# A windowed-attention stack on one core: TensorE's loop by half batches, products of 64 rows, k scaled by GpSimd

## The chip, the cores and the metric

One NeuronCore of a Trainium2 chip runs the whole program; the other cores are idle. The metric is the device time of one execution in microseconds, median of repeated runs. Everything is float32, except for a few bf16 operands in the first part and the masks.

## The reference

```python
x = L0_attn_x                                  # (8, 512, 128)
xn = _layernorm(x)
x + attn(xn) + stack(xn)

def stack(x):                                  # 6 layers
    for i in range(6):
        x = attn_layer(shift_tokens(x), Wqkv[i], q_scale[i], k_scale[i], Wo[i]) + x
        x = ffn_layer(shift_tokens(x), ...) + x

def attn_layer(x, Wqkv, qs, ksc, Wo):          # 16 heads of 64
    q, k, v = split(x @ Wqkv)
    q, k = l2norm(q) * qs, l2norm(k) * ksc     # t / max(norm, 1e-12)
    q = q * cos * scale + rotate_half(q) * sin * scale
    k = k * cos / scale + rotate_half(k) * sin / scale
    # queries of a window of 32 see the keys of their window and the one before
    return local_attention(q, k, v) @ Wo
```

`attn` is plain attention with 16 heads of 8 over 512 tokens. `ffn_layer` is a layer norm, a product to 2x341, an exact gelu gate and a product back to 128.

## The kernel before, in words

Four parts run one after another: a layer norm with transposes (`layer_norm_and_transpose`), the plain attention (`global_attention`, a hardware loop over pairs of its 32 tiles, L260), the windowed stack (`windowed_stack`) and the final sum (`add_up`). The change touches only the windowed stack.

The stack works in units. A unit is one batch of one layer, 512 tokens in TPB = 4 tiles of 128, so there are 48 units. Activations lie transposed in `xT`, 128 channels on the partitions. For a tile, TensorE makes q, k and v (L1023, two matmuls of 512 columns each), 1,024 columns a tile in a PSUM slot. ScalarE squares q and k (L889), GpSimd folds the squares in two (`fold`, L749), VectorE sums them and puts a floor under the norm (`norms`, L816 and L817), ScalarE makes the reciprocal root (`norm`, L939 and L944, event `rooted`). Meanwhile VectorE multiplies q and k by the cosine and sine tables (`rotate`, L796 and L798), GpSimd adds the two (`add_q`, `add_k`, L754), and VectorE scales the sum by the root (`scale_q`, `scale_k`, both L825). TensorE transposes (`qT`, `kT`, L977), ScalarE copies out (L907, L914). Scores of a tile (`s`) are a mask matmul (L982) and 64 matmuls of 64 rows (L992); VectorE takes the maximum off (L833, L834), ScalarE exponentiates (L918), TensorE transposes the probabilities (`r`, L977), ScalarE copies (L924).

The products with the values come in two stages a tile, `va` and `vb`, for the heads' two halves (L1004). `va` holds v in the tile's own windows, `vb` the same shifted by a window of 32 rows; transfers on SyncE's queue make `vb` from `va` (L717 to L721). Both have a second dimension of 2 that is zero outside of one half of the partitions, so that one matmul with all 128 rows gives two windows side by side, 2x65 columns (64 and a column of ones that sums the probabilities). VectorE divides (L842, L843), and once both are there transposes in blocks (`turn`, L850). After the fourth tile comes the unit's own work: `wo` (L1045), `residual` (L856), a token shift (L880 and on), `centre`, `var`, `z`, the three pairs `h` (L1056) with gelu gate and `hid` (L864), and `y` (L1060, then L868).

The order on each engine is written out by hand in strings, PE_ORDER, DVE_ORDER, ACT_ORDER, POOL_ORDER and SP_ORDER; a trailing "-" means the unit before. Four PSUM slots of two banks are shared by all stages by the table SLOTS_OF; a stage on TensorE waits until the slot's last user has been read. `units` unrolls each order in a first unit, a loop over the batches of the first layer (L665), and an outer loop over layers (L667) that holds the layer's first unit and a loop over the other seven (L670).

## Time and profile before

| | |
|---|---|
| median of 3 runs | 4115.5 us (4113.0 to 4125.6) |
| profiled execution | 4122.6 us |
| its span | 4120.8 us |
| busy: TensorE / VectorE / ScalarE / GpSimd | 3682.6 / 3501.6 / 2524.6 / 1584.2 us |
| mean granted TensorE clock | 0.974 |

Times are from the start of the span. Busy time of TensorE ("PE") is that of its matmuls; weight loads ("PEld") run beside them and each matmul of float32 stands as two records (a transpose as one). A bracket "[0.68 <-issue]" says how long the engine was idle ahead of the row and what ended it; "issue" is none of the other engines. A matmul row's duration reaches past the start of the next one, so costs are read from start to start.

### The profile page before, as it was taken

The page shows a single profiled execution, that of the slowest core. Times are in us where ns is not written, and L with a number is a line of the kernel's source. Part 1 is how long each engine was busy: PE and PEld are TensorE (multiplying, and loading weights), DVE is VectorE, ACT ScalarE, POOL GpSimd, SP SyncE. Part 2 cuts the span into 40 slices and gives each one's busy share as a digit, 9 for nine tenths or more (in the row PEclk, how much of TensorE's full clock was granted, in tenths as well). Part 3 has the DMA queues.
Part 4 walks back from the last instruction along what each step waited for, and adds up shares of the span by engine and source line. Part 5 has one row for each costly group of instructions (what it writes and reads, how often), then busy time and mean ns, then how long its engine had stood idle before and what let it go on. Part 6 is the DMA issues. An engine that isn't in the chain of part 4 may idle for free. (4 is left out here: it accounts for less than half of the span.)

```text
span 4120.8 us, 121950 instructions
## 1 busy us (share of the span) xinstructions
PE 3682.6 (89%) x49057; PEld 2078.7 (50%) x49312; DVE 3501.6 (85%) x4692; ACT 2524.6 (61%) x3292; POOL 1584.2 (38%) x1114
## 2 busy tenths in 40 slices
PE   5888885799998999998999989999989999899997
PEld 2333331455555555555555545555555555555554
DVE  6788885799898898898899889898879899789985
ACT  3666663465666565656666656666656666566663
POOL 3232231434343444444444434444434343344441
PEclk8999997899999999999999999999999999999998
DMA  1000001111112111112111111111121111111112
GB/s 27 1 1 1 1 1 57 41 37 25 37 25 52 36 32 30 35 28 58 27 36 30 33 53 32 31 34 29 31 58 25 37 25 37 51 32 31 32 31 57
DMA packets 60615, 131.31 MB, mean 32 GB/s; under 512 B 15748, under 2 KB 31624, under 8 KB 60168
## 3 DMA queue, kind: packets, MB, share of 16 engines
q1 hardware_dynamic: 60168, 124.11, 12.4%
q8 instruction: 432, 7.08, 0.7%
q14 instruction: 15, 0.12, 0.0%
HBM read 23.62 MB, written 4.19 MB: 7 GB/s over the span
## 5 line engine op out<-in xcount | busy, mean ns | idle before, releaser
L1023 PE MATMUL slot<-w_qkv,xs 128*128 (+1 forms) x2304 | 1108.3, 611 | 102.6 <-issue 73.4
L749 POOL TENSOR_TENSOR half_sq<-sq 128x1024 f32<-128x1024 f32 x192 | 501.2, 2610 | 1579.3 <-ACT sq L889 1569.7
L754 POOL TENSOR_TENSOR cosq<-cosq,sinq 128x1024 f32<-128x1024 f32 x384 | 901.9, 2365 | 362.9 <-DVE sinq L798 361.8
L1023 PEld LDWEIGHTS slot<-w_qkv,xs 128*128 128x128 f32 x2304 | 409.7, 193 | 523.2 <-issue 497.4
L889 ACT ACTIVATE sq<-slot 128x1024 f32<-128x1024 f32 x384 | 391.8, 1020 | 406.7 <-PE slot L1023 406.7
L796 DVE TENSOR_TENSOR cosq<-slot,table 128x1024 f32<-128x1024 f32 x384 | 467.3, 1217 | 195.3 <-ACT sq L889 182.7
L825 DVE TENSOR_TENSOR qk<-cosq,ry 128x1024 f32<-128x1024 f32 x384 | 473.5, 1244 | 0.6 <-ACT ry L944 0.6
L798 DVE TENSOR_TENSOR sinq<-slot,table 128x1024 f32<-128x1024 f32 x384 | 465.7, 1213 | 0.0
L977 PEld LDWEIGHTS slot<-ident,qk 128*128 128x128 f32 x3072 | 350.7, 142 | 226.7 <-issue 136.9
L977 PE MATMUL slot<-ident,qk 128*128 128x128 f32 x3072 | 396.8, 275 | 47.7 <-DVE qk L825 43.6
L373 DVE TENSOR_REDUCE at_rowmax<-at_slot 128x1 f32<-128x512 f32 x512 | 317.1, 683 | 51.8 <-PE at_slot L460 51.1
L1045 PE MATMUL slot<-oT,w_o 128*128 128x512 f32 x768 | 337.5, 592 | 2.5 <-DVE oT L850 2.5
L1004 PE MATMUL slot<-vb,probT 128*32 128x130 f32 x6144 | 322.8, 277 | 14.7 <-issue 6.8
L992 PE MATMUL slot<-kT,qT 64*32 64x64 f32 x24576 | 297.6, 225 | 34.0 <-issue 33.1
L426 ACT ACTIVATE at_probs<-at_slot 128x1024 f32<-128x1024 f32 x256 | 245.8, 1027 | 133.4 <-PE at_slot L474 133.3
L992 PEld LDWEIGHTS slot<-kT,qT 64*32 64x32 f32 x24576 | 258.7, 105 | 123.2 <-issue 123.2
L1004 PE MATMUL slot<-va,probT 128*32 128x130 f32 x6144 | 317.4, 273 | 2.9 <-issue 2.9
L843 DVE TENSOR_TENSOR o<-slot,rden 128x512 f32<-128x512 f32 x384 | 265.4, 691 | 13.2
L1056 PE MATMUL slot<-xs,w 128*114 128x512 f32 x576 | 273.2, 597 | 3.1 <-ACT xs L956 3.1
L901 ACT COPY va<-slot 64x1024 f32<-64x1024 f32 x192 | 192.4, 1002 | 135.3 <-PE slot L1004 126.5
L914 ACT COPY kT<-slot 128x1024 f32<-128x1024 f32 x192 | 194.4, 1012 | 101.3 <-PE slot L977 101.3
L1004 PEld LDWEIGHTS slot<-vb,probT 128*32 128x32 f32 x6144 | 166.5, 108 | 172.7 <-issue 166.5
(123 smaller groups left out, 5516.9 us busy)
## 6 DMA issues: line engine op xcount, KB each, us to landing
vb<-va SPq DMA_DIRECT2D x720, 130.0 KB, 2.3
w_qkv<-in_w_qkv SPq DMA_DIRECT2D x21, 512.0 KB, 4.8
w_o<-in_w_o SPq DMA_DIRECT2D x6, 512.0 KB
w<-in_w SPq DMA_DIRECT2D x6, 342.0 KB
res<-in_x SPq DMA_DIRECT2D x4, 512.0 KB, 6.0
kept<-res SPq DMA_DIRECT2D x1, 2048.0 KB, 8.7
out<-fin_res SPq DMA_DIRECT2D x8, 256.0 KB, 2.4
w<-in_w SPq DMA_DIRECT2D x6, 171.0 KB
```

Source lines behind the costliest of these rows:

```text
L373: nc.vector.reduce_max(rowmax[:, n:n + 1], slot("max", n)[:, :], AX.X).then_inc(S["max_read"], 1)
L749: nc.gpsimd.tensor_tensor(half_sq[:, :, :], squares[:, :, 0, :], squares[:, :, 1, :], ALU.add).then_inc(S["folded"], 1)
L754: nc.gpsimd.tensor_tensor(cosq[:, side], cosq[:, side], sinq[:, side], ALU.add).then_inc(S["qk"[side] + "_added"], 1)
L796: nc.vector.tensor_tensor(cosq[:, side].rearrange("p h a d -> p h (a d)"), ps.rearrange("p h a d -> p h (a d)"), cos[:, None, :].broadcast ...
L798: nc.vector.tensor_tensor(sinq[:, side], ps[:, :, ::-1, :], sin.rearrange("p (a d) -> p a d", a=2)[:, None, :, :].broadcast_to([P, HEADS, ...
L825: nc.vector.tensor_tensor(qk[:, side], cosq[:, side].rearrange("p h a d -> p h (a d)"), ry[:, side * HEADS:(side + 1) * HEADS, None].broad ...
L889: nc.scalar.activation(sq[:, "qk".index(name)].rearrange("p h d -> p (h d)"), flat(name, n), ACT.Square).then_inc(S[name + "_squared"], 1)
L977: last = nc.tensor.transpose(flat(kind, n)[:, c * P:(c + 1) * P], src[:, c * P:(c + 1) * P], ident[:, :])
L992: last = nc.tensor.matmul(slot("s", t)[32 * g:32 * g + 32, r, (4 * a + n) * DH:(4 * a + n + 1) * DH], qT[rows, c, tok:tok + WIN], kT[t % 2 ...
L1004: last = nc.tensor.matmul(slot(kind, t)[32 * g:32 * g + 32, r, 0:4 * PITCH].rearrange("p (w d) -> p w d", d=PITCH)[:, n::2, 0:VA], probT[: ...
L1023: last = nc.tensor.matmul(slot(kind, n)[:, i, :], xs[:, n * P:(n + 1) * P], w_qkv[:, (0 if layer is None else layer) % 2, "qkv".index(kind ...
L1045: last = nc.tensor.matmul(slot("wo")[:, 0, :], w_o[:, c, :], oT[:, :, a, :, r, half, :], start=c == 0, stop=c == QCH - 1)
```

## The change

- `va` and `vb` lose the dimension of zeros. Each product is now a matmul of 64 rows and 65 columns for one window pair's half; there are twice as many, and the two halves go to the two banks of the slot. ScalarE copies v in one instruction, a tile's `vb` takes one transfer of 96 rows and one of 32. Two tiles of buffers (VTILES) take the place of three.
- TensorE's loop runs over half batches (two tiles), nested in one loop over units. Work of the whole unit stands in the body with "first:" or "second:" and under a condition; so does each projection, whose tile depends on the half. The waits compute their values from the half. The unrolled first unit of a layer is gone on TensorE only.
- `scale_k` is GpSimd's. The norm's floor is a maximum with a tensor `least` that holds 1e-24, in place of a constant.
- All orders and the table of slots are new. In them "-" on TensorE means the half batch before.

```diff
-PE_ORDER = stages(
-    "q0 k0 qT3- kT3- r2- s3- vb2- k1 va2- kT0 q1 qT0 v0 r3- k2 va3- vb3- s0 q2 wo- qT1 r0 v1 kT1 centre- vb0 va0 "
-    "var- q3 v2 s1 k3 qT2 h0- kT2 h1- r1 h2- s2 vb1 v3 va1 y- ")
+PE_ORDER = half_stages(
+    "s0- q0 k0 second:wo- qT1- q1 second:centre- r0- second:var- kT1- va0- vb0- second:h0- second:h1- v0 "
+    "second:h2- s1- qT0 k1 kT0 second:y- r1- v1 va1- vb1- ")
 DVE_ORDER = stages(
-    "rotate_q0 rotate_k0 norms0 s3- scale_k0 vb2- scale_q0 va2- rotate_k1 turn2- rotate_q1 va3- vb3- turn3- "
-    "norms1 s0 scale_q1 rotate_q2 residual- scale_k1 rotate_k2 norms2 vb0 va0 scale_k2 scale_q2 z- rotate_q3 s1 "
-    "rotate_k3 turn0 hid0- norms3 hid1- hid2- s2 scale_q3 vb1 va1 scale_k3 turn1 y- ")
+    "vb1- va1- s2- rotate_q0 turn1- rotate_k0 norms0 va2- vb2- scale_q0 s3- rotate_q1 rotate_k1 turn2- vb3- va3- "
+    "norms1 turn3- s0 scale_q1 rotate_k2 residual- rotate_q2 norms2 z- va0 vb0 scale_q2 rotate_q3 hid0- turn0 "
+    "hid1- hid2- s1 rotate_k3 y- norms3 scale_q3 ")
...
 POOL_ORDER = stages(
-    "fold1- add_q1- add_k1- add_q2- fold2- add_k2- fold3- add_q3- add_k3- fold0 add_k0 add_q0 ")
+    "add_k1- scale_k1- fold2- add_k2- add_q2- add_q3- scale_k2- fold3- add_k3- scale_k3- fold0 add_q0 add_k0 "
+    "scale_k0 add_q1 fold1 ")
 SP_ORDER = stages(
-    "vb0 vb1 vb2 vb3 ")
+    "vb2- vb3- vb0 vb1 ")
 
 
 SLOTS_OF = (
-    "q0 r2 vb2 q1 vb3 q2 r0 centre k3 r1 va1",
-    "kT3 s3 kT0 qT0 r3 va3 s0 qT1 kT1 va0 v2 qT2 kT2 s2 y",
-    "k0 va2 v0 wo v1 s1 h1 vb1",
-    "qT3 k1 k2 vb0 q3 h0 h2 v3",)
+    "wo q1 h2 y v1",
+    "s0 qT1 r0 va0 h0 s1 r1",
+    "q0 kT1 v0 k1 vb1",
+    "k0 centre vb0 h1 qT0 kT0 va1",
+)
...
-          "q_scaled": ("dve", TPB), "k_scaled": ("dve", TPB), "probs": ("act", TPB),
+          "q_scaled": ("dve", TPB), "k_scaled": ("pool", TPB), "probs": ("act", TPB),
...
-VTILES = 3
+VTILES = 2
...
-        va = sb("va", [P, VTILES, 2, HEADS, VA])
-        vb = sb("vb", [P, VTILES, 2, HEADS, VA])
+        va = sb("va", [P, VTILES, HEADS, VA])
+        vb = sb("vb", [P, VTILES, HEADS, VA])
...
-            eng.wait_ge(vb_ready[t], 16 * VB_DMAS[t] * (unit + 2))
+            eng.wait_ge(vb_ready[t % 2], VB_UNIT[t % 2] * (unit + 1) + VB_UP_TO[t])
...
-            def align():
-
-                if order is PE_ORDER:
-                    eng.addr_align(FETCH)
             step(0, 0, 0, 0, False)
-            align()
             with eng.Fori(1, BATCH) as b:
                 step(b, 0, b, 1, True)
             with eng.Fori(1, DEPTH) as l:
                 step(l * BATCH, l, 0, BATCH, True)
-                align()
                 with eng.Fori(1, BATCH) as b:
                     step(l * BATCH + b, l, b, BATCH + 1, True)
             step(DEPTH * BATCH, None, BATCH, DEPTH * BATCH, False)
...
-                sp.dma_start(vb[32:64, s, 0, :, :], va[0:32, s, 0, :, :]).then_inc(vb_ready[t], 16)
-                sp.dma_start(vb[64:96, s, 1, :, :], va[32:64, s, 0, :, :]).then_inc(vb_ready[t], 16)
-                sp.dma_start(vb[96:128, s, 1, :, :], va[64:96, s, 1, :, :]).then_inc(vb_ready[t], 16)
+                sp.dma_start(vb[32:128, s, :, :], va[0:96, s, :, :]).then_inc(vb_ready[t % 2], 16)
                 if t:
-                    sp.dma_start(vb[0:32, s, 0, :, :], va[96:128, (t - 1) % VTILES, 1, :, :]).then_inc(vb_ready[t], 16)
+                    sp.dma_start(vb[0:32, s, :, :], va[96:128, (t - 1) % VTILES, :, :]).then_inc(vb_ready[t % 2], 16)
...
+                pool.memset(v[:, :, :, DH:VA], 1.0).then_inc(S["const_ready"], 1)
...
+                elif kind == "scale_k":
+                    wait(pool, "k_added", unit, t)
+                    wait(pool, "rooted", unit, t)
+
+                    wait_tile(pool, "kT_filled", unit, t)
+                    nc.gpsimd.tensor_tensor(qk[:, 1], cosq[:, 1].rearrange("p h a d -> p h (a d)"),
+                                            ry[:, HEADS:2 * HEADS, None].broadcast_to([P, HEADS, DH]),
+                                            ALU.mult).then_inc(S["k_scaled"], 1)
...
-                    nc.vector.tensor_scalar(ss[:, :], ss[:, :], 1e-24, None, ALU.max).then_inc(S["sumsq"], 1)
-                elif kind in ("scale_q", "scale_k"):
-                    side = ("scale_q", "scale_k").index(kind)
-                    name = "qk"[side]
-                    wait(dve, name + "_added", unit, n)
+                    nc.vector.tensor_tensor(ss[:, :], ss[:, :], least[:, :], ALU.max).then_inc(S["sumsq"], 1)
+                elif kind == "scale_q":
+                    wait(dve, "q_added", unit, n)
                     wait(dve, "rooted", unit, n)
 
-                    wait_tile(dve, name + "T_filled", unit, n)
-                    nc.vector.tensor_tensor(qk[:, side], cosq[:, side].rearrange("p h a d -> p h (a d)"),
-                                            ry[:, side * HEADS:(side + 1) * HEADS, None].broadcast_to([P, HEADS, DH]),
-                                            ALU.mult).then_inc(S[name + "_scaled"], 1)
+                    wait_tile(dve, "qT_filled", unit, n)
+                    nc.vector.tensor_tensor(qk[:, 0], cosq[:, 0].rearrange("p h a d -> p h (a d)"),
+                                            ry[:, 0:HEADS, None].broadcast_to([P, HEADS, DH]),
+                                            ALU.mult).then_inc(S["q_scaled"], 1)
...
-                    ps = slot(kind, n)[:, :, 0:4 * PITCH].rearrange("p r (w d) -> p r w d", d=PITCH)
+                    ps = slot(kind, n)[:, :, 0:4 * VA].rearrange("p v (s d) -> p v s d", d=VA)
                     link(nc.vector.reciprocal(rden[:, a], ps[:, :, :, DH]), kind)
-                    nc.vector.tensor_tensor(o[:, a].rearrange("p w r d -> p r w d"), ps[:, :, :, 0:DH],
+                    nc.vector.tensor_tensor(o[:, a].rearrange("p (v n) r d -> p v (n r) d", v=2), ps[:, :, :, 0:DH],
                                             rden[:, a, :, :, None].broadcast_to([P, 2, 4, DH]), ALU.mult).then_inc(S[kind + "_read"], 1)
...
-                    old, unit_of = (0, unit) if n == VTILES else ((TPB - 1 if n == 0 else n), unit - 1)
+                    old, unit_of = (n - VTILES) % TPB, unit + (n - VTILES) // TPB
...
-                    nc.scalar.copy(va[0:DH, n % VTILES, 0, :, 0:DH], ps[0:DH])
-                    nc.scalar.copy(va[DH:P, n % VTILES, 1, :, 0:DH], ps[DH:P]).then_inc(S["v_read"], 1)
+                    nc.scalar.copy(va[:, n % VTILES, :, 0:DH], ps).then_inc(S["v_read"], 1)
...
                 return last
 
-            def products(kind, t):
+            def products(kind, n):
                 a = ("va", "vb").index(kind)
                 for r in range(2):
-                    for n, values in enumerate((vb, va)):
+                    for m, values in enumerate((vb, va)):
                         for g in range(4):
-
-                            last = nc.tensor.matmul(
-                                slot(kind, t)[32 * g:32 * g + 32, r, 0:4 * PITCH].rearrange("p (w d) -> p w d", d=PITCH)[
-                                    :, n::2, 0:VA],
-                                probT[:, 4 * r + 2 * a + n, 32 * g:32 * g + 32],
-                                values[:, t % VTILES, :, 2 * (4 * a + g) + r, :],
-                                start=True, stop=True, skip_group_check=True)
+                            for v in range(2):
+                                rows = slice(DH * v, DH * v + DH)
+
+                                last = nc.tensor.matmul(
+                                    slot(kind, n)[32 * g:32 * g + 32, v, (2 * m + r) * VA:(2 * m + r + 1) * VA],
+                                    probT[rows, 4 * r + 2 * a + m, 32 * g:32 * g + 32],
+                                    values[rows, n, 2 * (4 * a + g) + r, :],
+                                    start=True, stop=True, skip_group_check=True)
                 return last
 
...
-                    for i in range(2):
-                        last = nc.tensor.matmul(slot(kind, n)[:, i, :], xs[:, n * P:(n + 1) * P],
-                                                w_qkv[:, (0 if layer is None else layer) % 2, "qkv".index(kind), i * SEQ:(i + 1) * SEQ], start=True, stop=True)
+
+                    def project(half):
+                        for i in range(2):
+                            last = nc.tensor.matmul(slot(kind, n)[:, i, :], xs[:, (2 * half + n) * P:(2 * half + n + 1) * P],
+                                                    w_qkv[:, layer % 2, "qkv".index(kind), i * SEQ:(i + 1) * SEQ],
+                                                    start=True, stop=True)
+                        last.then_inc(S[kind + "_filled"], 1)
+                    if isinstance(h, int):
+                        project(h)
+                        return
+                    with pe.If(1 - h):
+                        project(0)
+                    with pe.Else():
+                        project(1)
+                    return
...
-                    wait_vb(pe, unit, n)
+                    wait_tile_of("r_read", u, h, n, back)
+                    value = lambda half: VB_UNIT[n] * ((half - back) // 2 + 1) + VB_UP_TO[2 * ((half - back) % 2) + n]
+                    pe.wait_ge(vb_ready[n], VB_UNIT[n] * u + by_half([value(0), value(1)], h))
                     passed(pe)
                     last = products(kind, n)
...
-            units(pe, PE_ORDER, stage)
+
+            def half_step(u, h):
+
+                known = isinstance(u, int)
+                layer = u // BATCH
+                at = 0
+                while at < len(PE_ORDER):
+                    kind, n, back, only = PE_ORDER[at]
+                    if only is None:
+                        if not known or 0 <= 2 * u + h - back < 2 * UNITS:
+                            wait_slot(at, u, h)
+                            tile_stage(kind, n, back, u, h, layer)
+                        at += 1
+                        continue
+                    run = at
+                    while run < len(PE_ORDER) and PE_ORDER[run][3] == only:
+                        run += 1
+
+                    def chunk():
+                        for i in range(at, run):
+                            kind, n, back, _ = PE_ORDER[i]
+                            if not known or 0 <= u - back < UNITS:
+                                wait_slot(i, u, only)
+                                unit_stage(kind, n, u - back)
+                    if not known:
+                        with pe.If(h if only else 1 - h):
+                            chunk()
+                    elif h == only:
+                        chunk()
+                    at = run
+            for h in range(2):
+                half_step(0, h)
+            pe.addr_align(FETCH)
+            with pe.Fori(1, UNITS) as u:
+                with pe.Fori(0, 2) as h:
+                    half_step(u, h)
+            for h in range(2):
+                half_step(UNITS, h)
```

TensorE, the end of its inner loop over batches (L1023 projections, L977 transposes, L992 scores, L1004 products, L1060 y, L670 the loop). Before:

```order
L1004 MATMUL slot<-vb,probT 32x2x65 x4
L1004 MATMUL slot<-va,probT 32x2x65 x4
L1004 MATMUL slot<-vb,probT 32x2x65 x4
L1004 MATMUL slot<-va,probT 32x2x65 x4
L1060 MATMUL slot<-hid,w 128x512 x3
L670 REGISTER_ALU
L670 COMPARE_AND_BRANCH
L667 REGISTER_ALU
```

Now, y and the end of the half-batch body (L1074 projections, L984 transposes, L1013 products, L1128 y, L1155 a condition, L1164 and L1163 the two loops; the projection stands twice, for the one half and the other):

```order
L1155 COMPARE_AND_BRANCH
L1035 REGISTER_ALU
L144 ISA
L1128 MATMUL slot<-hid,w 128x512 x3
L1155 UNCONDITIONAL_BRANCH
L984 MATMUL slot<-ident,prob 128x128 x8
...
L1013 MATMUL slot<-vb,probT 32x65 x8
L1013 MATMUL slot<-va,probT 32x65 x8
L1164 REGISTER_ALU
L1164 COMPARE_AND_BRANCH
L1163 REGISTER_ALU
L1163 COMPARE_AND_BRANCH
```

The loop's end stood behind y; it now stands behind the products of a tile, y is under a condition of its own.

VectorE, at the third tile's norm (L816 reduce, L817 floor, L842 and L843 outputs, L825 scale_k and scale_q, L860 z). Before:

```order
L816 TENSOR_REDUCE ss<-half_sq 128x32
L806 REGISTER_ALU
L817 TENSOR_SCALAR ss<-ss 128x32
L842 RECIPROCAL rden<-slot 128x8
L843 TENSOR_TENSOR o<-slot,rden 128x2x4x64
L842 RECIPROCAL rden<-slot 128x8
L843 TENSOR_TENSOR o<-slot,rden 128x2x4x64
L825 TENSOR_TENSOR qk<-cosq,ry 128x1024 x2
L860 TENSOR_TENSOR xs<-slot,sqc 128x512
```

Now, the same tiles' norm with what follows (L826 reduce, L827 floor, L868 z, L850 and L851 outputs, L833 scale_q):

```order
L826 TENSOR_REDUCE ss<-half_sq 128x32
L816 REGISTER_ALU
L827 TENSOR_TENSOR ss<-ss,least 128x32
L868 TENSOR_TENSOR xs<-slot,sqc 128x512
L850 RECIPROCAL rden<-slot 128x8
L851 TENSOR_TENSOR o<-slot,rden 128x512
L850 RECIPROCAL rden<-slot 128x8
L851 TENSOR_TENSOR o<-slot,rden 128x512
L833 TENSOR_TENSOR qk<-cosq,ry 128x1024
```

The floor became a tensor-tensor instruction with two inputs, and one of the two scalings, scale_k, is gone from behind the outputs.

GpSimd, the end of its loop (L749 or L751 fold, L754 or L764 add, L758 scale_k). Before:

```order
L749 TENSOR_TENSOR half_sq<-sq 128x1024
L754 TENSOR_TENSOR cosq<-cosq,sinq 128x1024 x2
L135 ISA
L749 TENSOR_TENSOR half_sq<-sq 128x1024
L754 TENSOR_TENSOR cosq<-cosq,sinq 128x1024 x2
L670 REGISTER_ALU
L670 COMPARE_AND_BRANCH
```

Now:

```order
L751 TENSOR_TENSOR half_sq<-sq 128x1024
L764 TENSOR_TENSOR cosq<-cosq,sinq 128x1024 x2
L758 TENSOR_TENSOR qk<-cosq,ry 128x1024
L144 REGISTER_ALU
L764 TENSOR_TENSOR cosq<-cosq,sinq 128x1024
L751 TENSOR_TENSOR half_sq<-sq 128x1024
L675 REGISTER_ALU
L675 COMPARE_AND_BRANCH
```

A scale_k follows each add_k, and a fold with an add is left over at the end.

## Rows read from the trace of the kernel before

**Rows 1.** The page's part 1: busy time, share, instructions.

```profile
PE 3682.6 (89%) x49057; PEld 2078.7 (50%) x49312; DVE 3501.6 (85%) x4692; ACT 2524.6 (61%) x3292; POOL 1584.2 (38%) x1114
```

**Rows 2.** One line of the code, the y stage: duration min/median/max, first and last start.

```profile
L868 DVE SCALAR_TENSOR_TENSOR xT<-slot,vec,x x48: 705/708/751, 852.0 to 4099.9; 128x512 f32 x42, 128x512 f32<-128x512 f32 x6
```

**Rows 3.** Table by stretches: length, then busy us by engine, clock, DMA, GB/s.

```profile
2001.57:2069.36 67.79, 64.12 (x948) 37.55 (x951) 60.51 (x66) 43.26 (x57) 28.25 (x12) 1.00 0.14 32
...
1817.00:1961.00 144.00, 128.15 (x1870) 75.88 (x1878) 120.02 (x133) 83.82 (x112) 58.27 (x24) 0.98 0.19 48
```

**Rows 4.** TensorE's timeline in one inner unit: start, us, line, out<-in, count [idle before].

```profile
2005.48 0.43 PE L1004 MATMUL slot<-vb,probT 128*32 128x130 f32 x8
...
2007.39 1.12 PE L1052 MATMUL slot<-sqc,ones 128*128 128x512 f32 x2
...
2012.01 0.38 PE L982 MATMUL slot<-mask,ident 128*128 128x512 bf16 x1
2012.32 1.49 PE L992 MATMUL slot<-kT,qT 64*32 64x64 f32 x128
2013.73 1.98 PE L1023 MATMUL slot<-w_qkv,xs 128*128 x4
2015.55 1.04 PE L977 MATMUL slot<-ident,qk 128*128 128x128 f32 x8
2016.42 1.88 PE L1056 MATMUL slot<-xs,w 128*114 128x512 f32 x4
...
2025.91 0.33 PE L992 MATMUL slot<-kT,qT 64*32 64x64 f32 x11 [0.68 <-issue]
...
2030.33 2.84 PE L1060 MATMUL slot<-hid,w 114*128 114x512 f32 x6
2033.87 3.67 PE L1023 MATMUL slot<-w_qkv,xs 128*128 x8 [0.69 <-issue]
...
2061.62 7.03 PE L1045 MATMUL slot<-oT,w_o 128*128 128x512 f32 x16
2068.49 1.04 PE L977 MATMUL slot<-ident,qk 128*128 128x128 f32 x8
```

**Rows 5.** Loop branches on TensorE's queue; DMA queues of two inner units, then of 200:640.

```profile
L670 PEldq COMPARE_BRANCH  x35: 82/3397/3917, 1404.8 to 4049.9; - x35
...
L260 PEldq COMPARE_BRANCH  x15: 76/208/241, 104.4 to 645.5; - x15
...
q8 instruction: 18, 0.29, 0.9%
...
q1 hardware_dynamic: 1173, 0.28, 0.3%
```

**Rows 6.** TensorE's timeline past a layer boundary, columns as in rows 4.

```profile
1895.02 5.14 PE L1023 MATMUL slot<-w_qkv,xs 128*128 x8 [7.67 <-issue]
```

**Rows 7.** Groups by line over the span: shapes and count | busy us, mean ns | idle before.

```profile
L754 POOL TENSOR_TENSOR cosq<-cosq,sinq 128x1024 f32<-128x1024 f32 x384 | 901.9, 2365 | 362.9 <-DVE sinq L798 361.8
...
L817 DVE TENSOR_SCALAR ss<-ss 128x32 f32<-128x32 f32 x192 | 200.8, 1046 | 6.7
```

**Rows 8.** Single lines of VectorE, columns as in rows 2.

```profile
L825 DVE TENSOR_TENSOR qk<-cosq,ry x384: 1210/1215/2727, 718.5 to 4051.6; 128x1024 f32<-128x1024 f32 x192
...
L817 DVE TENSOR_SCALAR ss<-ss x192: 180/1323/1400, 716.6 to 4042.9; 128x32 f32<-128x32 f32 x192
```

**Rows 9.** Timelines of GpSimd and VectorE at two places, columns as in rows 4.

```profile
1021.03 2.36 POOL L754 TENSOR_TENSOR cosq<-cosq,sinq 128x1024 f32<-128x1024 f32 x1 [6.49 <-DVE sinq L798]
...
1023.04 1.42 DVE L825 TENSOR_TENSOR qk<-cosq,ry 128x1024 f32<-128x1024 f32 x1
...
1023.34 3.35 POOL L749 TENSOR_TENSOR half_sq<-sq 128x1024 f32<-128x1024 f32 x1
...
2004.70 2.36 POOL L754 TENSOR_TENSOR cosq<-cosq,sinq 128x1024 f32<-128x1024 f32 x1 [0.31 <-DVE sinq L798]
...
2005.78 1.32 DVE L817 TENSOR_SCALAR ss<-ss 128x32 f32<-128x32 f32 x1
```

123 lines of the change are left out of this document (81 added, 42 removed), and 6 rows, old and new, of the table ACT_ORDER.

## The prediction

> **What bounds the kernel now.** The page's busy line comes first [rows 1]: TensorE 89% and VectorE 85% of the span, ScalarE 61%, GpSimd 38%. Two engines near full, neither of them full, says that each waits for the other in turn. The y stage's row gives the beat of the windowed stack [rows 2]: 48 units between 852.0 and 4099.9 us, so 3247.9/47 = 69.1 us a unit. All of the change lies in these 48 units. The table by stretches [rows 3] splits this: a unit inside a layer takes 67.8 us, two units across a layer boundary 144.0, some 8 us more than two inner ones. In the inner unit TensorE is busy 64.1 of 67.8 us, VectorE 60.5, ScalarE 43.3, GpSimd 28.3.
>
> A row's duration overstates TensorE, since matmuls overlap; its cost is read from start to next start in its timeline [rows 4]. Both product stages of a tile: 2005.48 to 2007.39, 1.91 us (1.95 below, as the mean of the two forms they take). Scores of a tile: 1.41, with the mask 1.75. A projection takes 1.75 to 1.82 (1.75 in most places), eight transposes 0.87, wo 6.87; the feed-forward's other stages, read likewise, 10 together. The unit's sum is 12x1.75 + 12x0.88 + 4x1.75 + 4x1.95 + 6.87 + 10 = 63 us, beside 64.1 busy in the table. So TensorE has 5 us of air in a unit of 68.
>
> Two holes of this air come with the releaser "issue", thus no engine made it wait: 0.68 us inside the scores at 2025.91, and 0.69 us before the first projection after the loop's branch at 2033.87 [rows 4]. The branch's own row says why [rows 5]: COMPARE_BRANCH at L670 takes 3.4 us in the median when it is taken, while y's 2.84 us of queued matmuls hide most of it. The loop of global attention (L260) has the same branch, and there it takes 0.21 us. The instruction queue moved 18 packets in two units of the stack, 9 each, and none at all between 200 and 640 us, in the attention loop (that window's DMA answer has the one line of queue 1) [rows 5]. So a short loop stays loaded and a loop of about 1,920 matmuls and weight loads doesn't. At the boundary the same thing opens a hole of 7.67 us [rows 6].
>
> **The change, part by part.** (1) Products. A tile's 32 matmuls of 128 rows and 130 columns become 64 of 64 rows and 65 columns. The nearest row is the scores stage: 64 matmuls of 64 rows, 32 columns of weights and 64 moving columns, 1.41 us [rows 4]. I take 1.45 for 65 columns; so 1.95 - 1.45 = 0.5 us a tile, **2.0 us a unit** off TensorE, sum 61 us. The bounds: half the time of before (0.98), or as much per matmul as now (1.91/32 = 0.06 us, so 3.8).
>
> (2) TensorE's loop by half batches. Its body holds 6x16 transposes, 2x260 for scores, 4x128 for products, 24x4 for projections of both branches and 76 for the feed-forward, some 1,300 matmuls and weight loads, against about 1,920. I take it to stay loaded as the attention loop does: the two holes (1.4 us here) go, and the boundary's extra 8 us shrinks to about 2, which is 5x6 = 30 us in all or **0.6 us a unit**. Executed instructions rise from 1,920 to about 2,430 a unit. Twelve conditional branches stand in each half, at 0.21 us taken [rows 5]. Those behind a projection hide under its 1.75 us; those behind scores or products (q0, v0, the back edge) do not. I charge 0.4 us a unit; bounds 0 and 24x0.21 = 5.0.
>
> (3) scale_k leaves VectorE: four instructions of 1.22 us [rows 8], about 1.14 from start to start, **4.6 us a unit**. GpSimd takes four of about 2.37 [rows 7], 28.3 + 9.5 = 38 us a unit, which is still not the bound.
>
> (4) The norm's floor. TENSOR_SCALAR at L817 has a mean of 1.05 us [rows 7], a median of 1.32 and a minimum of 0.18 [rows 8]. The timeline shows why [rows 9]: at 2005.78 it starts while GpSimd's add (2004.70 to 2007.06) runs, and it ends with that add. If the tensor-tensor form is free of this it costs 0.18 and saves 0.87x4 = 3.5 us a unit. But a tensor-tensor with both inputs in SBUF already stands in the trace, qk<-cosq,ry at L825. At 1023.04 it starts with 0.35 us left of an add and takes 1.42 instead of 1.21 us; the fold that GpSimd issued at 1023.34 takes 3.35 instead of 2.37, as it waits for VectorE in turn. At the start, with a whole add ahead of it, L825 took 2.73 us, the maximum of its row [rows 8]. The new floor reads ss and least, both in SBUF, and follows a fold in whose wake the next add starts. So I book **no gain**; bounds 0 and 3.5. The Trainium skill (SBUF — State Buffer, "Who interferes with whom") has this as a rule: a VectorE instruction with two SBUF inputs contends with a GpSimd one that reads SBUF. The rows of L825 agree. By the opposite reading the sum would be the fast rival's below.
>
> (5) scale_q. GpSimd now has 16 instructions a unit in place of 12, and add_k and scale_k stand just where scale_q is issued. By the same rows scale_q waits for the running one. Bounds: nothing, as in its median of today, and a whole 2.37. I take 0.7 each, **+2.8 us a unit**. VectorE's net is then -4.6 + 2.8 = -1.8, some 59 us a unit.
>
> (6) The copy of v is one of 128 partitions in place of two of 64; 15 transfers a unit become 7 with the same bytes. I cost both at nothing: ScalarE has 24 us of air in a unit [rows 3], and the values are used half a batch later. If ScalarE were late, the slots of qT, kT and v would be next.
>
> **The sum, walked along the new orders.** Halves are unequal. In the first TensorE has 22.2 us of work and VectorE two tiles, 22 us before waits. In the second the feed-forward brings TensorE to 39 and VectorE to 31. I walked both queues, with the waits of the code and these durations. First half, in us from the end of q0: rotate_k0 frees its slot at 7.2; norms0 is held by GpSimd's adds until 10.0; va and vb until 11.7; scale_q0 waits for scale_k0 and ends at 14.0. TensorE's qT0 could have begun at 12.6. s3 then ends at 16.4, rotate_q1 at 18.7, and the next q0 ends at 25.4: 3.2 us over TensorE's own 22.2. The second half is TensorE's own, 39, plus about 1.5 us: it waits for wo's residual, z and v's turn of the slots. Together 65.9 us, with branches 66.3. Boundaries add 2x5/47 = 0.2. So 66.5 against 69.1 us: -2.6x47 = -122, and about 10 us less for the ends of the stack where the same holes stand. The profiled execution took 4122.6 us, 1.8 over its span and 7.1 over the median of the runs; 4122.6 - 132 = 3990, which on the median's footing is 3984. I say **3985 us**.
>
> **The rivals.** *Fast: GpSimd doesn't hold VectorE.* Either the tiny floor slips through, or its start falls between two GpSimd instructions, and so with scale_q. The same walk without these waits (norms0 over at 7.8, scale_q0 at 10.6) has the next q0 end at 22.5 and the unit at 62.3; with branches and boundaries 62.9: -6.2x47 = -291, so about 3830. For it: a quarter of the floors take 0.18 us already ((1.32 - 1.05)/(1.32 - 0.18)), and the new order may bring it to more. Against it: GpSimd is now busy 38 of 66 us, up from 28 of 68.
>
> *Slow: the code does not stay loaded.* The attention loop shows about 400 matmuls and weight loads that stay; nothing in the trace shows 1,300. If the half loop is loaded anew each time, a unit has two back edges of 3.4 us in place of one, and each stands behind vb1's short products and not behind y. That is 6.8 us less some 1.5 of walked waits that they cover; four stretches of scores and products, each longer than the one that has today's hole of 0.41 to 0.68 us, add 2.2 us. 66.5 + 7.5 = 74 us, +4.9x47 = +230, about 4350. It decides from the point where a taken branch takes over 2 us. The Trainium skill (Runtime: NRT & Kernel Launch, "Instruction fetch mechanics") has a rule to this effect, a taken branch whose target is outside of a two-page window stalls for a fetch; by that window the unit would take this rival's 74 us. The same section gives TensorE's instruction memory 2,048 places, and by that the half loop fits and the forecast's 66.5 us stand. The trace of before has the stall of 3.4 us, and can't tell the two.
>
> *Slow, in small: branches or small matmuls.* With no branch hidden the unit is 65.9 + 5.0 + 0.2 = 71.1 us, +2.0x47 = +94, 4210. If a matmul of 64 rows costs what one of 128 does now, TensorE rises by 4x1.9 = 7.6 us instead of falling by 2.0, which is more. Against both: the scores stage, and register instructions between stages that leave no hole today.
>
> **The numbers.** The forecast, with waits of scale_q between a third and twice what I took and branches up to 2 us, holds 3900 to 4100: 0.54. Fast rival: 0.27. Code not loaded: 0.08. Branches or matmuls: 0.07. Gains that cancel: 0.04. The range of 8 in 10 is **3830 to 4100**; half of the fast rival reaches below its middle, and its low end is drawn at that middle. A measurement tells 0.3% from no change, 12 us. Faster by more 0.82, within 0.03, slower 0.15.
>
> **What would show it.** Starts of y 66 to 67 us apart, and no longer unit at the boundary. Both products of a tile start to start in 1.4 to 1.6 us. No packets on the instruction queue in the stack and back edges near 0.2 us; 3 us and 12 to 14 packets a unit would be the slow rival. The floor's row still near 1.1 us in the mean, scale_q's at 1.6 to 2.2; floors at 0.18 and scale_q at 1.22 would be the fast one. TensorE's holes mostly in front of qT, released by scale_q. The forecast is wrong if the unit is under 64 or over 68.5 us.

## The result: slower, and the profile after

The changed kernel takes 4217.9 us in the median (4210.4 to 4218.4, 4 runs) where the kernel before takes 4120.6 beside it (4113.0 to 4125.6, 4 runs): a ratio of **1.023, 95% interval 1.022 to 1.0246**. The forecast was 3985 us and the range ended at 4100. It was wrong, in sign too.

The page's busy line and the y stage's row, after, answer to [rows 1, 2]:

```profile
PE 3592.9 (85%) x61345; PEld 2038.8 (48%) x61600; DVE 3327.3 (79%) x4500; ACT 2328.1 (55%) x3100; POOL 1991.5 (47%) x1305
```

```profile
L876 DVE SCALAR_TENSOR_TENSOR xT<-slot,vec,x x48: 749/751/752, 839.0 to 4195.5; 128x512 f32 x42, 128x512 f32<-128x512 f32 x6
```

Units start (4195.5 - 839.0)/47 = 71.4 us apart, against 69.1. None stands out at a layer boundary any more: all but the last are 71.5 to 71.7 us long. Before, six of a layer's eight were near 68.2 us, the next 70.3 and the one across the boundary 79.0. TensorE, VectorE and ScalarE are all less busy than before, and the kernel is slower: the time went into gaps, not into work.

The table by stretches has one unit in its two halves, and answers to [rows 3] (columns as there):

```profile
2137.08:2164.91 27.83, 23.39 (x586) 15.31 (x589) 25.86 (x28) 14.48 (x18) 15.90 (x7) 1.00 0.11 32
2164.91:2208.73 43.82, 40.09 (x625) 22.51 (x627) 32.04 (x36) 25.31 (x36) 21.74 (x9) 1.00 0.09 25
```

The walk gave these halves 25.4 and 40.5 us: 2.4 and 3.3 short. The granted clock is full in both. TensorE is busy 63.5 of 71.65 us, so it stands still for 8.2; in the unit of [rows 3] that was 67.8 - 64.1 = 3.7. TensorE's timeline says what it stands still for. These are all its holes over 0.2 us of that unit, and at 2141.49 the place where a projection follows a transposes stage without one (columns as in [rows 4]):

```profile
2141.49 1.88 PE L1074 MATMUL slot<-w_qkv,xs 128*128 x4
...
2145.71 0.32 PE L1013 MATMUL slot<-vb,probT 64*32 64x65 f32 x13 [0.59 <-ACT probT L931]
...
2147.70 1.98 PE L1074 MATMUL slot<-w_qkv,xs 128*128 x4 [0.38 <-issue]
2150.45 0.38 PE L989 MATMUL slot<-mask,ident 128*128 128x512 bf16 x1 [0.77 <-issue]
...
2153.08 1.06 PE L984 MATMUL slot<-ident,qk 128*128 128x128 f32 x8 [0.83 <-DVE qk L833]
...
2157.90 1.98 PE L1074 MATMUL slot<-w_qkv,xs 128*128 x4 [0.27 <-DVE sinq L808]
...
2162.34 0.38 PE L989 MATMUL slot<-mask,ident 128*128 x1 [0.90 <-issue]
...
2164.91 3.69 PE L1074 MATMUL slot<-w_qkv,xs 128*128 x8 [0.70 <-issue]
...
2176.79 1.98 PE L1074 MATMUL slot<-w_qkv,xs 128*128 x4 [0.44 <-DVE x L864]
...
2183.80 0.33 PE L1013 MATMUL slot<-vb,probT 64*32 64x65 f32 x13 [0.69 <-DVE xs L868]
...
2201.37 1.98 PE L1074 MATMUL slot<-w_qkv,xs 128*128 x4 [0.69 <-issue]
...
2206.19 0.38 PE L989 MATMUL slot<-mask,ident 128*128 x1 [1.28 <-issue]
2208.71 0.69 PE L1074 MATMUL slot<-w_qkv,xs 128*128 x1 [0.56 <-issue]
```

Seven holes end with "issue", 5.28 us together. One of them, the 0.77 at 2150.45, is not what it says. The queue's row at L634 shows a wait on a semaphore there (queue rows: duration min/median/max ns, first and last start):

```profile
L634 PEldq EVENT_SEMAPHORE  x1: 1541/1541/1541, 2148.6 to 2148.6; - x1
```

It ends at 2150.2, just after VectorE's normalising of the slot that the scores take over (o at L851 ends at 2150.13). The other six, 0.38 + 0.90 + 0.70 + 0.69 + 1.28 + 0.56 = **4.51 us a unit**, are the queue's own. Five of them follow products or scores, the stages of short matmuls, and one follows transposes. In the unit of [rows 4] "issue" had 0.68 + 0.69 = 1.4. Over the 36 units in the middle of the span, "issue" has 5.3 us a unit, so this unit is a typical one.

What fills the longest of them, 1.28 us in front of 2206.19 where both loops end, is in the queue's rows of 2204.5 to 2206.19. In the order of their starts they are the inner loop's addition and branch (2204.6, 2204.7), the outer's (2204.8, 2204.9), a move for each (2205.2, 2205.3), and from 2205.4 four pieces for registers and a semaphore:

```profile
L1164 PEldq ALU_OP  x1: 36/36/36, 2204.6 to 2204.6; - x1
L1164 PEldq COMPARE_BRANCH  x1: 67/67/67, 2204.7 to 2204.7; - x1
...
L1163 PEldq ALU_OP  x1: 36/36/36, 2204.8 to 2204.8; - x1
L1163 PEldq COMPARE_BRANCH  x1: 209/209/209, 2204.9 to 2204.9; - x1
...
L1164 PEldq FUSED_REGOPS  x1: 138/138/138, 2205.4 to 2205.4; - x1
...
L1027 PEldq FUSED_REGOPS  x1: 68/68/68, 2205.6 to 2205.6; - x1
...
L634 PEldq EVENT_SEMAPHORE  x1: 51/51/51, 2205.7 to 2205.7; - x1
...
L989 PEldq FUSED_REGOPS  x1: 69/69/69, 2205.8 to 2205.8; - x1
```

Ten records of 0.74 us in sum take 1.3 us from start to end: on a queue too, the cost of a record is its start to the next one's, and its duration is little more than half of that.

Over the whole span the queue's rows are these. L1081 holds the conditions around projections, L1155 those around the stages of one half, L1163 and L1164 the two loops; L1027 and L1035 are registers worked out for waits:

```profile
L1155 PEldq COMPARE_BRANCH  x564: 63/138/224, 775.0 to 4129.9; - x188
...
L1081 PEldq COMPARE_BRANCH  x846: 63/169/324, 773.3 to 4135.1; - x170
...
L1163 PEldq COMPARE_BRANCH  x47: 67/209/209, 844.0 to 4139.0; - x47
...
L1164 PEldq COMPARE_BRANCH  x94: 67/142/223, 800.1 to 4138.8; - x94
...
L1027 PEldq FUSED_REGOPS  x376: 67/73/73, 768.7 to 4134.9; - x188
...
L1035 PEldq FUSED_REGOPS  x376: 72/73/108, 775.8 to 4134.8; - x188
```

That is (564 + 846 + 47 + 94)/47 = 33 branch records a unit, near 0.15 us each, where the kernel before had one of 3.4 us behind y. None is longer than 0.33 us, and the instruction queue moved 20 packets in the whole span:

```profile
q8 instruction: 20, 0.33, 0.0%
```

So the half loop does stay loaded, as forecast, and the rival "the code does not stay loaded" is out. The page of before has 432 such packets.

### The profile page after: what moved, and what is told of

Its sections match the earlier page's. It is cut to its first block and busy times, and to the rows that moved or that the text cites. A ratio compares the mean times of both kernels' runs of the same rounds, so it can differ in the third digit from the quotient of the medians.

```text
span 4216.4 us, 150009 instructions
## 1 busy us (share of the span) xinstructions
PE 3592.9 (85%) x61345; PEld 2038.8 (48%) x61600; DVE 3327.3 (79%) x4500; ACT 2328.1 (55%) x3100; POOL 1991.5 (47%) x1305
## 5 line engine op out<-in xcount | busy, mean ns | idle before, releaser
L764 POOL TENSOR_TENSOR cosq<-cosq,sinq 128x1024 f32<-128x1024 f32 x384 | 904.3, 2361 | 789.3 <-DVE sinq L808 789.2
L1074 PE MATMUL slot<-w_qkv,xs 128*128 (+1 forms) x2304 | 1101.2, 607 | 167.7 <-issue 111.5
L751 POOL TENSOR_TENSOR half_sq<-sq 128x1024 f32<-128x1024 f32 x192 | 453.7, 2363 | 590.6 <-ACT sq L897 383.6
L1074 PEld LDWEIGHTS slot<-w_qkv,xs 128*128 128x128 f32 x2304 | 405.3, 191 | 571.8 <-issue 571.7
L758 POOL TENSOR_TENSOR qk<-cosq,ry 128x1024 f32<-128x1024 f32 x192 | 460.3, 2397 | 260.7 <-ACT ry L951 182.9
L984 PE MATMUL slot<-ident,qk 128*128 128x128 f32 x3072 | 402.4, 274 | 53.4 <-DVE qk L833 47.4
L984 PEld LDWEIGHTS slot<-ident,qk 128*128 128x128 f32 x3072 | 351.1, 141 | 191.3 <-issue 160.4
L1013 PE MATMUL slot<-vb,probT 64*32 64x65 f32 x12288 | 277.6, 227 | 62.6 <-DVE xs L868 32.4
L833 DVE TENSOR_TENSOR qk<-cosq,ry 128x1024 f32<-128x1024 f32 x192 | 276.1, 1438 | 46.4 <-ACT ry L951 46.4
L841 DVE TENSOR_REDUCE smax<-slot 128x16 f32<-128x1024 f32 x192 | 232.2, 1209 | 98.5 <-PE slot L999 98.5
L1013 PEld LDWEIGHTS slot<-vb,probT 64*32 64x32 f32 x12288 | 220.7, 105 | 166.4 <-issue 160.0
L1013 PE MATMUL slot<-va,probT 64*32 64x65 f32 x12288 | 283.3, 223 | 1.7 <-issue 1.7
L851 DVE TENSOR_TENSOR o<-slot,rden 128x512 f32<-128x512 f32 x384 | 265.4, 691 | 13.2
L909 ACT COPY va<-slot 128x1024 f32<-128x1024 f32 x192 | 193.8, 1010 | 147.1 <-PE slot L1013 121.1
```

The lines of the kernel that those rows point to most:

```text
L751: nc.gpsimd.tensor_tensor(half_sq[:, :, :], squares[:, :, 0, :], squares[:, :, 1, :], ALU.add).then_inc(S["folded"], 1)
L758: nc.gpsimd.tensor_tensor(qk[:, 1], cosq[:, 1].rearrange("p h a d -> p h (a d)"), ry[:, HEADS:2 * HEADS, None].broadcast_to([P, HEADS, DH] ...
L764: nc.gpsimd.tensor_tensor(cosq[:, side], cosq[:, side], sinq[:, side], ALU.add).then_inc(S["qk"[side] + "_added"], 1)
L984: last = nc.tensor.transpose(flat(kind, n)[:, c * P:(c + 1) * P], src[:, c * P:(c + 1) * P], ident[:, :])
L1013: last = nc.tensor.matmul(slot(kind, n)[32 * g:32 * g + 32, v, (2 * m + r) * VA:(2 * m + r + 1) * VA], probT[rows, 4 * r + 2 * a + m, 32 * ...
L1074: last = nc.tensor.matmul(slot(kind, n)[:, i, :], xs[:, (2 * half + n) * P:(2 * half + n + 1) * P], w_qkv[:, layer % 2, "qkv".index(kind), ...
```

## The experiments

Twelve kernels ran, each in three rounds against the kernel before. The last column is the y row's first to last start over 47, from each one's own trace; before it is 69.1 and with the whole change 71.4. The whole change ran in a round of its own, and the kernel before had medians from 4111.0 to 4121.9 us beside the different runs, so a difference between runs of two rounds is uncertain by some 10 us.

| run | what is different | time, us | ratio to before, 95% | us a unit |
|---|---|---|---|---|
| a_noif | change, no condition at projections | 4147.2 | 1.0075 [1.0058, 1.0092] | 70.0 |
| a_moreif | change, 12 more conditions, ahead of projections | 4283.0 | 1.0408 [1.0389, 1.0428] | 72.8 |
| a_ifbehind | change, the same 12, behind projections | 4213.7 | 1.0233 [1.0205, 1.0262] | 71.5 |
| a_unroll | change, both halves written out | 4375.5 | 1.0638 [1.062, 1.0656] | 74.9 |
| a_reg | change, 24 more waits | 4233.9 | 1.0306 [1.0284, 1.0327] | 71.8 |
| a_reg2 | change, 24 more waits on values of their own | 4254.1 | 1.0329 [1.03, 1.0358] | 72.3 |
| a_128 | change, products of before | 4241.0 | 1.032 [1.0299, 1.0341] | 72.1 |
| a_floor | change, floor of before | 4217.8 | 1.0251 [1.0234, 1.0268] | 71.4 |
| a_kdve | change, scale_k on VectorE | 4251.1 | 1.0336 [1.0315, 1.0358] | 72.2 |
| b_kpool | before, scale_k on GpSimd | 4139.0 | 1.0056 [1.0039, 1.0072] | 69.5 |
| b_64 | before, products of the change | 4289.2 | 1.044 [1.0409, 1.0472] | 72.7 |
| b_flat | before, TensorE's loop over 47 units | 4069.5 | 0.9892 [0.9872, 0.9912] | 68.0 |

### Conditions on TensorE's queue

**a_noif** takes the condition at each projection away; the second half then projects the first two tiles again, so its output is not the reference's.

```diff
-                    with pe.If(1 - h):
-                        project(0)
-                    with pe.Else():
-                        project(1)
+                    project(0)
```

> The changed kernel with the condition around the projections taken away: both halves project the first two tiles of the batch, so the second half's own tokens are left out of the computation; the number and shape of matmuls stay. Theory C: 6 of 12 conditions a half go, among them the exposed ones before q0 and v0; -2 to -3 us a unit, about 4090 to 4120. Theory P: VectorE is busy 25.9 of 27.8 us in the first half anyway, so less than -0.5 us a unit, 4195 to 4220.

**a_moreif** puts one more condition, which guards a bare semaphore increment, ahead of each projection's own.

```diff
+                    with pe.If(h):
+                        passed(pe)
                     with pe.If(1 - h):
                         project(0)
```

> The changed kernel with one more condition ahead of each projection on TensorE: 6 more in a half batch, 12 in a unit, each with a counter's step inside. Theory C (TensorE's conditions and register work are what costs): a condition takes 0.1 to 0.3 us of its queue and about half of them stand where nothing hides them, so 12 x 0.15 = 1.8 us a unit, 47 units, +85 us: about 4300. Theory P (VectorE and GpSimd holding each other bound the unit): TensorE's queue has air, 0 to +20 us, 4220 to 4240.

Measured: 12 conditions fewer save 71 us, 1.5 us a unit by the medians; 12 more cost 65, 1.4 a unit. The second run is the cleaner: its trace has 12 more branch records a unit, 1.6 us of queue, and 6 semaphore records. In the first, 18 of the 33 branch records go and 12 of the 53 fused register records with them, so it takes both away together. By the second a condition ahead of a projection costs near 0.12 us, about what it takes on the queue. The matmuls do not hide it. The remaining question is why not, since the prediction had argued that a projection's 1.75 us hides anything.

**a_ifbehind** has the same twelve, moved behind the projection's matmuls:

```diff
                     with pe.Else():
                         project(1)
+                    with pe.If(h):
+                        passed(pe)
                     return
```

> The changed kernel with the same 12 conditions a unit more as in the run that put them ahead of each projection (which cost 65 us), but behind each projection's matmuls, ahead of whatever stage follows. Theory Q (a condition costs only where TensorE's queue has no lead; a projection's four matmuls take 1.75 us, so behind one there is a lead): 0 to 0.5 us a unit, 4215 to 4245 us. Rival (a condition costs its 0.12 us wherever it stands): +1.4 us a unit, 4275 to 4290 us.

Measured: 4213.7 us and the ratio of the change itself, 1.0233. Twelve conditions that cost 65 us in front of a projection cost nothing behind one. Both traces have the same 45 branch records a unit with the same durations. The price of a condition thus depends on what the queue has in hand when it comes, which the rates of the rows would explain: behind the four of a projection (1.75/4 = 0.44 us each; the trace has each matmul of the code as two) there is a lead, behind the 128 of scores (1.41/128 = 0.011 us each) there is none. In front of a half's six projections stand scores or products twice, transposes of 0.87 us three times, and a projection once. In the timeline above, the projection at 2141.49 follows transposes and starts without a hole, the one at 2147.70 follows products and has 0.38.

**a_unroll** writes both halves out in the unit's body: no conditions and no registers for h, but twice the code.

```diff
-                    if not known:
+                    if not known and not isinstance(h, int):
...
-                with pe.Fori(0, 2) as h:
+                for h in range(2):
```

> The changed kernel with the loop over the two halves written out, so the unit's body has no condition at all, but some 2,650 instructions that do not stay loaded. Theory C: the 5.8 us of idle time a unit that end in 'issue' go; loading comes back with one back edge of 3.4 us and holes of 0.5 us in the dense stretches, 2 to 4 us a unit; net -2 to -3 us a unit, about 4090. Theory L (loading the code is worse than the conditions): 12 loads a unit and holes in each stretch of scores and products, +1 to +3 us a unit, 4260 to 4350. Theory P: as now within 0.5 us a unit, if both are hidden behind VectorE.

This is the worst of all, 4375.5 us. The page has 530 instruction packets, and the loop's branch and the hole behind it read:

```profile
q8 instruction: 530, 8.68, 0.9%
```

```profile
L1163 PEldq COMPARE_BRANCH  x47: 79/3920/6033, 836.6 to 4286.1; - x47
```

```profile
2191.37 0.63 PE L989 MATMUL slot<-mask,ident 128*128 128x512 bf16 x1 [4.55 <-issue]
```

The holes of conditions are gone from the middle of the unit, and 4.55 us stand behind the branch, since here short products and not y's long matmuls are queued ahead of it. The hole has a second price. TensorE does nothing in it, and towards its end the granted clock falls to the lower of its two levels, 1.2 GHz, here from 2190.0 to 2196.8, and likewise once in every unit; in the changed kernel it is full in all inner units (first the row of 7 us by stretches, columns as in [rows 3], then two projections):

```profile
2191.00:2198.00 7.00, 6.49 (x135) 3.80 (x137) 2.45 (x2) 0.47 (x1) 0.00 (x0) 0.59 0.04 13
```

```profile
2194.29 4.92 PE L1074 MATMUL slot<-w_qkv,xs 128*128 x8
```

From 2191.37 to the end of these two at 2199.05, mask, scores and projections take 7.7 us. At full clock they take 1.7 (2012.01 to 2013.73 in [rows 4]) and 3.5 (2137.08 to 2140.61 above). So an estimated 2.4 of the 3.4 us by which this kernel's inner unit is longer than the changed one's are the clock's; "issue" holes grow as well, from 5.3 to 7.1 us a unit in the mean. The half loop's conditions are the cheaper of the two ills. But before, the loop's branch had y to hide behind.

### Waits and registers

**a_reg** repeats the stage's own wait ahead of transposes, scores and products, for instance:

```diff
                     wait_tile_of("probs", u, h, n, back)
+                    wait_tile_of("probs", u, h, n, back)
```

> The changed kernel with one more wait, on a value that TensorE works out from its two loop registers and that is always met already, ahead of each transpose and scores stage and of each va and vb: 24 more a unit, no condition. Theory R (register work costs TensorE time, not the conditions alone, as some 53 register operations of 0.08 us a unit in the queue suggest): 0.05 to 0.1 us each, +1.2 to +2.4 us a unit, 4275 to 4330 us. Rival (only conditions cost, register operations and waits hide under matmuls): within 0.3 us a unit, 4205 to 4232 us.

It costs 16 us by the medians, but it does not test what it was meant to. Its trace has the same 53 fused register operations a unit as the change and 10 more semaphore records: the repeated values were shared. So **a_reg2** asks for values of their own, 3u + h, 2u + 3h and so on:

```diff
+                    pe.wait_ge(S[name], of_u * u + of_h * h)
```

> The changed kernel with one more wait ahead of each transpose, scores and product stage, each against a value of its own (3u+h, 3u+2h, 2u+h and so on, always met already): 12 in the half loop, so 24 more register operations and 24 more waits a unit, and no condition. The trace of the changed kernel has 53 fused register operations of 0.08 us a unit on TensorE's queue. Theory R (register work costs as it stands in the queue, above all behind short matmuls): 24 x 0.08 = 1.9 us a unit at most, half of it at least: 4260 to 4310 us. Theory C (a condition, with its jump, is what costs, 0.12 us each; plain register work hides): +0.2 to +0.6 us a unit, 4225 to 4250 us.

Measured: 4254.1 us, +36, or 0.8 us a unit. Its trace has 24 more register records a unit (6 fused, 18 plain of 0.04 us) and 4 more semaphore records, 1.1 us in all. The result lies between the two expectations, and a little nearer to the second: register work is not free, but a piece of it costs 0.03 us where a condition cost 0.12.

### The products

**a_128** has the change with the old products (32 matmuls of 128 rows a tile), the old va and vb, copies and transfers.

```diff
-                            for v in range(2):
-                                rows = slice(DH * v, DH * v + DH)
...
-                                    probT[rows, 4 * r + 2 * a + m, 32 * g:32 * g + 32],
-                                    values[rows, n, 2 * (4 * a + g) + r, :],
...
+                                probT[:, 4 * r + 2 * a + m, 32 * g:32 * g + 32],
+                                values[:, n, :, 2 * (4 * a + g) + r, :],
```

> The changed kernel with the products, va, vb, the copy of v and the transfers of the kernel before (32 matmuls of 128 rows a tile in place of 64 of 64 rows; two tiles of each buffer); loop, orders and scale_k as changed. From start to next start of another stage, products take 9.82 us a unit in the changed kernel and 9.34 before, though a tile's alone went from 1.95 to 1.5. Theory Q (TensorE takes short matmuls about as fast as its queue hands them over, so behind 64 of them the queue has no lead, and each condition or register behind them opens a hole; 32 long ones give it a lead again): the products' 0.45 us a tile longer are mostly made up by smaller holes behind them, the unit 71.2 to 72.2 us, 4200 to 4245 us. Rival A (the matmuls themselves bound these stages and the holes stay): +0.45 x 4 = 1.8 us a unit, 4290 to 4310 us.

Measured: +23 us by the medians, +0.7 us a unit over all 47, not 1.8. An inner unit is only 0.4 longer (72.05 against 71.66); the unit across a layer boundary is 73.8, and the last one 67.4 against 61.6. Why these two kinds are longer stays open. The timeline of one unit (2129.5 to 2201.5) has these "issue" holes, the one at 2150.93 again a semaphore's:

```profile
2130.74 1.98 PE L1077 MATMUL slot<-w_qkv,xs 128*128 x4 [0.68 <-issue]
2135.17 0.60 PE L994 MATMUL slot<-mask,ident 128*128 x2 [0.54 <-issue]
2137.75 3.70 PE L1077 MATMUL slot<-w_qkv,xs 128*128 x8 [0.56 <-issue]
...
2150.93 0.59 PE L994 MATMUL slot<-mask,ident 128*128 128x512 bf16 x2 [0.65 <-issue]
...
2165.44 3.69 PE L1077 MATMUL slot<-w_qkv,xs 128*128 x8 [0.75 <-issue]
...
2195.63 1.98 PE L1077 MATMUL slot<-w_qkv,xs 128*128 x4 [0.28 <-issue]
```

The other five sum to 2.81 us in place of 4.51. The hole where both loops end, behind products, shrank from 1.28 to 0.54 (2206.19 above, 2135.17 here), though the same records stand there, and the one at the end of the inner loop, 0.90 at 2162.34 above, is gone. So of the 1.8 us that short products save, 0.4 is left in an inner unit, and most comes back as holes right behind them: they leave the queue no lead.

**b_64** is the same question asked of the kernel before: the new products, copy and transfers in the old unit loop.

```diff
-                    for n, values in enumerate((vb, va)):
+                    for m, values in enumerate((vb, va)):
                         for g in range(4):
+                            for v in range(2):
+                                rows = slice(DH * v, DH * v + DH)
```

> The kernel before, with the products by 64 rows, va and vb as one plain buffer of three tiles each, and 7 transfers a unit in place of 15: the half-batch loop, orders and scale_k stay as before. TensorE's body has 256 more matmuls and weight loads a unit (2,180 against 1,920). Theory P (short products save 0.45 us a tile on TensorE, and in the unit loop most of it reaches the end): 67 to 68 us a unit, 4020 to 4080 us. Rival L (a loop of this length is loaded anew, and what is added is loaded too: 13% more code): products 0.4 us shorter a tile but issue holes that give it back, 69 to 70 us a unit, 4110 to 4170 us.

Both expectations were too mild: 4289.2 us, +175. Its expectation also undercounts the code: each of the 128 matmuls more stands there as two, with two weight loads, so 512 instructions come on top of 1,966. The page has 528 instruction packets, 96 more. Two holes of one unit show where that comes through, the first behind the loop's branch (0.69 in [rows 4]), the second between the two products of a tile:

```profile
2103.44 3.67 PE L1019 MATMUL slot<-w_qkv,xs 128*128 x8 [1.19 <-issue]
```

```profile
2168.46 0.34 PE L1001 MATMUL slot<-va,probT 64*32 64x65 f32 x13 [1.56 <-issue]
```

"Issue" sums to 3.6 us in that unit, against 0.7 in the unit of before at the same place (2102 to 2170). Waits for VectorE and ScalarE grew as well, from 2.0 to 4.4 us, and its scaling of q and k takes 1.46 us in the mean in place of 1.24, since it meets GpSimd more often. The granted clock was at 1.2 GHz for 85 us between the first and the 47th y, against 44 before, which at half speed would explain 20 us of the 175 at most. How far one brought the other was not separated. So in the long loop the short products cost 4%, as more code to load and with longer waits; in the short one they are worth 23 us of the 85 (47 x 1.8) that they save in themselves, since they take the lead that hides the control.

### scale_k and the floor

**a_floor** puts the old form of the floor into the change:

```diff
-                    nc.vector.tensor_tensor(ss[:, :], ss[:, :], least[:, :], ALU.max).then_inc(S["sumsq"], 1)
+                    nc.vector.tensor_scalar(ss[:, :], ss[:, :], 1e-24, None, ALU.max).then_inc(S["sumsq"], 1)
```

> The changed kernel with the norm's floor as tensor-scalar with a constant again. Theory P as in the prediction (either form waits for GpSimd's running instruction): same time within 0.3%, the floor's mean duration 1.0 to 1.1 us. Rival (the tensor-tensor form is what keeps it short): the floor gets longer by 0.3 us or more and the time rises by 0.3 to 1%.

4217.8 us: no difference. **a_kdve** has scale_k back on VectorE in the changed kernel, **b_kpool** has it on GpSimd in the kernel before. Their orders change likewise for every tile; here a line of VectorE's order in a_kdve, then GpSimd's in b_kpool:

```diff
-    "vb1- va1- s2- rotate_q0 turn1- rotate_k0 norms0 va2- vb2- scale_q0 s3- rotate_q1 rotate_k1 turn2- vb3- va3- "
+    "vb1- va1- s2- rotate_q0 turn1- rotate_k0 norms0 va2- vb2- scale_q0 scale_k0 s3- rotate_q1 rotate_k1 turn2- vb3- va3- "
```

```diff
-    "fold1- add_q1- add_k1- add_q2- fold2- add_k2- fold3- add_q3- add_k3- fold0 add_k0 add_q0 ")
+    "fold1- add_q1- add_k1- scale_k1- add_q2- fold2- add_k2- scale_k2- fold3- add_q3- add_k3- scale_k3- fold0 add_k0 add_q0 "
+    "scale_k0 ")
```

> The changed kernel, with scale_k back on VectorE (behind each scale_q) and gone from GpSimd; everything else stays. VectorE is busy 25.9 of the 27.8 us of a first half. Theory C (TensorE's conditions and register work cost the change its gain, and moving scale_k helped): VectorE gets 4 x 1.22 us more a unit; the first half, in which it has the least air, grows by 1.5 to 2.4 us, the second by less than 1; a unit of 73 to 74 us, 4290 to 4350 us in all. Theory G (scale_k on GpSimd is what hurts, since add_q and the folds now queue behind it and VectorE waits for the adds): a unit of 69 to 70.5 us, 4100 to 4170 us, floors and scale_q of VectorE shorter in the mean.

> The kernel before, with scale_k on GpSimd alone of all the change: VectorE has 4.6 us less a unit, GpSimd 9.5 more. Theory C: this part helps, since in the kernel before VectorE ends what TensorE waits for in most of its holes (2.3 us a unit): 68 to 68.8 us a unit, 4060 to 4105 us. Theory G: scale_k takes 2.4 us on GpSimd where VectorE needed 1.2, its tile's transposes come later and scale_q waits for GpSimd: 70 to 72 us a unit, 4160 to 4250 us.

a_kdve costs 33 us more than the change, so the move to GpSimd is worth 0.8 us a unit there: theory C's sign, and less than half of its size. Its "issue" holes sum to 5.25 us in a unit, against 5.28 with the move, so the control's price doesn't depend on this. b_kpool costs 25 us more than before, and the groups of its trace say why (shapes and count | busy us, mean ns | idle before):

```profile
L834 DVE TENSOR_TENSOR qk<-cosq,ry 128x1024 f32<-128x1024 f32 x192 | 405.8, 2114 | 2.3 <-POOL cosq L763 2.3
...
L757 POOL TENSOR_TENSOR qk<-cosq,ry 128x1024 f32<-128x1024 f32 x192 | 366.2, 1907 | 325.4 <-issue 291.9 <-POOL cosq L763 32.0 <-ACT ry L953 0.7
```

scale_q takes 2.11 us where it took 1.24: it is issued together with scale_k and waits for it. In addition the transposes of k wait for GpSimd, with a hole of 1.50 us in front of them, in place of the 0.88 they waited for VectorE. In the changed kernel, whose order sets the two apart, the same instruction takes 1.44:

```profile
L833 DVE TENSOR_TENSOR qk<-cosq,ry 128x1024 f32<-128x1024 f32 x192 | 276.1, 1438 | 46.4 <-ACT ry L951 46.4
...
L827 DVE TENSOR_TENSOR ss<-ss,least 128x32 f32<-128x32 f32 x192 | 204.3, 1064 | 6.6
```

### The layer boundary, and a version faster than both

**b_flat** leaves everything of the kernel before and lets TensorE loop over 47 units, in place of a written first unit and a loop of 7 for each layer:

```diff
-            units(pe, PE_ORDER, stage)
...
+            flat_step(0, 0, False)
+            pe.addr_align(FETCH)
+            with pe.Fori(1, UNITS) as u:
+                flat_step(u, 1, True)
+            flat_step(UNITS, UNITS, False)
```

> The kernel before, with TensorE's loop flat over 47 units in place of a first unit written out for each layer and an inner loop of 7 (TensorE's code of the stack is two units shorter, each unit has 2 more register operations and the waits for the weights). Theory L (the long units at the layer boundaries come from loading code that was written out and isn't in the loop): all units 67.8 to 68.5 us apart, none of 76 at a boundary, 47 x 68.1 against 3247.9: 4060 to 4090 us. Rival (the boundary waits for the weights of the next layer or the tables, whatever the code): boundary pairs stay at 144 us, 4110 to 4130 us.

Measured: 4069.5 us, ratio 0.989: faster than both kernels, by 44 us than before and by 148 than the change.

```profile
L868 DVE SCALAR_TENSOR_TENSOR xT<-slot,vec,x x48: 705/708/751, 853.5 to 4047.1; 128x512 f32 x42, 128x512 f32<-128x512 f32 x6
```

No unit is longer than 69.1 us, so the long ones at the boundary came from TensorE's written-out code and not from weights or tables. But for the most part they did not come from loading it, as its expectation and the prediction have it. b_flat moves 434 instruction packets, as many as the kernel before with its 432. The kernel before also has `align()` inside the loop over layers, which pads the code ahead of the inner loop with `addr_align(FETCH)` (L662), and TensorE's queue runs the padding at every boundary (before, 1880 to 1900 us):

```profile
L662 PEldq NOP  x147: 13/13/13, 1883.9 to 1894.6; - x147
```

That is 147 instructions that do nothing, 73 ns from start to start, 10.7 us at each of five boundaries. The first of them pass under y's matmuls, the others fill the hole of 7.67 us in [rows 6] but for its last 0.3, and from 1884 to 1904 us no instruction packet moved at all. Within this hole, too, the granted clock falls to 1.2 GHz, for 6.8 us from 1891.15: the two projections of [rows 6] take 5.0 us from start to start in place of 3.5. b_flat pads once, ahead of its one loop, and has none of this. It takes the written-out unit and the padding away together; no run took the padding alone.

The inner units rise a little, from 68.2 to 68.5 us, which eats some of the gain. Of the parts of the change that were tried alone in the kernel before, this is the only one that pays, and it needs no half batches.

## Why the prediction was wrong

**What bounds the kernel.** The reading that TensorE and VectorE wait for each other in turn, with little air, held. That TensorE's own queue is a third party was seen in [rows 5] and then priced far too low. What that queue does at a layer boundary was misread: the hole of [rows 6] is not "the same thing" as the branch's, but padding.

**(1) Products: right in size, wrong as a gain.** Both products of a tile go from 1.95 to 1.5 us. Taken alone that is 1.8 us a unit (2.0 was booked). Added up from each matmul's start to the next matmul's, with the holes behind a stage in it, a unit's stages compare as follows (four inner units of each, the products' line L1004 before, L1013 after, and so on):

| us a unit | before | after |
|---|---|---|
| projections | 21.7 | 22.4 |
| transposes | 11.7 | 13.3 |
| scores with masks | 7.8 | 9.5 |
| products | 9.3 | 9.8 |
| wo to y | 17.8 | 16.7 |
| sum | 68.3 | 71.6 |

The products take half a microsecond more than before, holes behind them counted.

**(2) The half loop: this is the step that failed.** That the code stays loaded and the boundary's extra goes was right: 20 packets, and no long unit. The second was right by luck: the extra was for the most part the padding in the loop over layers, which the changed TensorE code no longer has there, and it was worth 5 x 12.9 = 65 us where 30 was booked. "I charge 0.4 us a unit; bounds 0 and 24x0.21 = 5.0" was the error. The queue's holes are 4.5 us a unit, 4.1 more than was charged, and the inner unit came out at 71.65 where 66.3 was walked. The rest of that, 1.2 us, is the balance of two others: engines made TensorE wait 3.6 us (8.1 of holes less 4.5) where the walk had 4.7, and it was busy for 63.5 us where the walk had 61.2. Busy time counts the last matmul before a hole to its end, which the next stage overlaps where there is no hole, so more holes also make a busier TensorE; that these are the whole 2.3 us was not shown. Nor are the 4.1 us fully taken apart: a_noif gives back 1.5, with conditions and registers together, and how the rest divides between registers, loop ends and the lead that short products take rests on the rows, a_reg2 and a_128. Two things were missed. The argument that a condition hides under the projection's 1.75 us looked at the matmuls that follow it, and a_ifbehind and a_moreif show that only those queued ahead of it count. And the registers for waits, which left no hole before, were taken over as free, though the half loop has 53 fused ones a unit where before had 3, and shorter matmuls to hide them behind.

**(3), (5) scale_k and scale_q.** The terms were -4.6 and +2.8 us a unit on VectorE. The first is its work, and busy time fell by 3.4 us between a_kdve and the change (61.3 to 57.9). scale_q's wait is 0.2 us each in the changed order, 0.9 a unit where 2.8 was booked, and 0.87 each in b_kpool's. At the end the move of scale_k was worth 0.8 us a unit with the new orders and cost 0.4 with the old.

**(4) The floor: right.** Mean 1.06 us against 1.05, and a_floor shows no gain. The rows of L827 and [rows 9] agree with the rule of the Trainium skill (SBUF — State Buffer, "Who interferes with whom"): the tensor-tensor form reads two SBUF inputs and waits for GpSimd. The old form took as long, so the conversion neither helps nor hurts. The fast rival is out with it: its floors did not slip through (minimum 0.19, median 1.08 us). Its scale_q nearly did, at 1.44 us in the mean, and the unit grew all the same.

**(6)** v's copy and transfers at nothing was right: no hole of the unit shown waits for them.

**The walk** fell short by 2.4 us in the first half and 3.3 in the second. The queue's holes in them are 0.38 + 0.90 + 0.70 = 1.98 and 0.69 + 1.28 + 0.56 = 2.53 us, of which it had 0.4 in all; its dependences were otherwise nearly right.

**The ends of the stack** were booked at -10 us and came out at +2.6: the first y starts 13.0 us earlier (839.0 for 852.0), and the last unit takes 61.6 us where it took 46.0. With them the whole adds up: 46 units x 3.46 (71.66 for 68.2) - 65 for the boundaries + 2.6 = +97 us, as measured.

**The rival that came true** is "branches not hidden", 4210 us, at 7 in 100. That a condition costs its full duration was right for the place where they stand. That its total comes within 8 us of the measured one is luck in part: it had 24 conditions at 0.21 us, 5.0 a unit, where one measured 0.12, which makes 2.9, and it had nothing for registers or for the second loop; its unit of 71.1 is near 71.65 because these and other terms fill the difference. The weight was wrong: the kernel before had no condition in its stack, so nothing spoke for hidden ones but the single branch behind y, whose cover of 2.84 us the short stages don't have. Of the two readings of the Trainium skill (Runtime: NRT & Kernel Launch, "Instruction fetch mechanics"), the window that would have made the unit 74 us does not show: a half loop with some 1,400 instructions moves no packets, as by the 2,048 places of the same section. But the loops of 1,966 move 9 packets each time around, though that figure would hold them; there the measurement decides.

## What to carry to other kernels

Count what stands on an engine's queue between its short instructions, not only the instructions: a condition or a register operation is hidden by the work queued ahead of it, never by what follows. Put conditions behind long matmuls. When a stage is cut into many short matmuls, most of its gain can be paid back where control follows it, and in a loop too long to stay loaded it is paid as code. Look at the queue's own records before a hole that ends with "issue" is given a cause: at the layer boundary they were 147 padding instructions, and one flat loop, without them and the written-out unit, was worth 1.1%. And count the work behind a long hole at the clock that its rows show.

## What was not expected of the hardware

Twelve conditions cost 65 us or nothing, by their side of a projection. A loop of 1,966 instructions moved 432 packets and one of 2,478 moved 528; over 48 units that is 9 and 11 a unit, and the half loop moves none. A padding instruction took 73 ns of TensorE's queue, and 147 of them stood in every layer boundary. In holes of 4.55 us (a_unroll) and 7.67 us (before), with TensorE idle, the granted clock fell to 1.2 GHz and stayed there for some 7 us. And of scale_q on VectorE and scale_k on GpSimd, the one that starts second waits for the other, whichever it is. Two places of the changed kernel's timeline (columns as in [rows 9]):

```profile
2149.95 1.90 POOL L758 TENSOR_TENSOR qk<-cosq,ry 128x1024 f32<-128x1024 f32 x1 [0.70 <-POOL cosq L764]
```

```profile
2150.89 2.04 DVE L833 TENSOR_TENSOR qk<-cosq,ry 128x1024 f32<-128x1024 f32 x1
```

VectorE's starts 0.9 us later, ends 1.1 us after GpSimd's end at 2151.85, and takes 2.04 us in place of 1.22.

```profile
2168.42 1.23 DVE L833 TENSOR_TENSOR qk<-cosq,ry 128x1024 f32<-128x1024 f32 x1 [0.18 <-ACT ry L951]
```

```profile
2168.55 2.86 POOL L758 TENSOR_TENSOR qk<-cosq,ry 128x1024 f32<-128x1024 f32 x1 [3.89 <-ACT ry L951]
```

Here GpSimd's starts 0.13 us later and takes 2.86 us, its 1.90 and most of VectorE's 1.23.
